# A recurrent layer with routed experts on one core: three groups of transposes declared float32r, with a float32r identity

## The reference, cut to what matters

```python
xn = _layernorm(x, axis=-1)
s = _L0_attn_ref(xn, ...)      # x@Wx -> conv -> silu -> b, c, dt -> scan -> norm -> * silu(z) -> @Wout
g = _silu(_L0_ffn_ref(xn, ...))
x = x + s * g

# inside _L0_attn_ref, with 8 heads of 64 and a state of 64 x 64 each
decay = jnp.exp(dt_t * a)[..., None, None]
state = decay * state + b_bar[..., None] * x_t[:, :, None, :]
y_t = jnp.einsum('bhn,bhnp->bhp', c_t, state)

# inside _L0_ffn_ref, with 8 experts, each taking its own top 1024 of 8192 tokens
G_t, idx_t = jax.lax.top_k(Sm.T, k)
tokens = xf[idx]
mid = jax.nn.silu(jnp.einsum('keh,ehf->kef', tokens, Wu) + bu)
out = jnp.einsum('kef,efh->keh', mid, W_down) + b_down
y = jnp.zeros_like(xf).at[idx].add(G[..., None] * out)
```

## Time and profile before

| | |
|---|---|
| Median of 3 runs | 1216.25 us (1212.61 to 1216.72) |
| The profiled execution | 1207.71 us, span 1205.9 us |
| TensorE busy | 1181.9 us, 98%, 13979 matmul records |
| Weight loads (PEld) | 973.4 us, beside the matmuls |
| VectorE, GpSimd, ScalarE busy | 79%, 64%, 54% |
| Start of the first transpose | 9.05 us (its weight load) |
| End of GpSimd's first wait in phase_front | 9.57 us |
| DMA | 214.84 MB, mean 178 GB/s |

### The profile page before, as it was taken

How to read it: one execution, slowest core, us unless ns; L and a number is a source line. 1 busy time by engine, 2 the same in 40 slices (tenths; PEclk the granted TensorE clock), 3 DMA queues, 4 the chain that set the end, 5 groups by cost and what they waited for, 6 DMA issues and landing times.

```text
span 1205.9 us, 35027 instructions
## 1 busy us (share of the span) xinstructions
PE 1181.9 (98%) x13979; PEld 973.4 (81%) x13979; DVE 947.5 (79%) x2272; ACT 653.2 (54%) x1406; POOL 774.4 (64%) x726
## 2 busy tenths in 40 slices
PE   9999999999999999999999998999999999999998
PEld 4566668888888878888878787888888888899998
DVE  7999975899987778777778778987767676777676
ACT  5999985454445444444444445455445443545444
POOL 4888945555455667666766658566766645577674
PEclk9999999999999999999999999999999999999999
DMA  9698774544343444443443346555544436799994
GB/s 304 242 360 324 281 277 133 115 154 122 132 148 124 149 126 122 134 144 120 131 140 129 120 126 199 159 151 97 119 92 106 81 80 133 272 333 318 333 333 164
DMA packets 122450, 214.84 MB, mean 178 GB/s; under 512 B 22448, under 2 KB 80560, under 8 KB 117552
## 3 DMA queue, kind: packets, MB, share of 16 engines
q1 hardware_dynamic: 109136, 195.32, 48.1%
q0 software_dynamic: 12288, 17.05, 8.4%
q10 hardware_dynamic: 864, 0.24, 0.1%
HBM read 131.03 MB, written 81.53 MB: 176 GB/s over the span
## 4 chain that ended last, share of the span: by engine, by line
PE 85%; DVE 5%; ACT 2%; DMA 2%; issue 2%; SPq 1%; POOL 1%; ACTq 0%; POOLq 0%; DVEq 0%
PE ps L1406 27%; PE ps L1772 10%; PE ps L2282 8%; PE ps L2261 7%; PE ps L2046 6%; PE ps L1496 3%; PE ps L1418 3%; PE ps L2048 3%; PE ps L1485 3%; PE ps L1473 3%; PE ps L1508 2%; PE ps L1428 2%; PE ps L682 2%; PE ps L630 2%; DMA x_dram<-x 1%
## 5 line engine op out<-in xcount | busy, mean ns | idle before, releaser
L1956 POOL DMA_INDIRECT ffn_dram<-ob,idx x64 | 108.6, 1697 | 83.5 <-DVE ob L1875 68.3
L1356 ACT ACTIVATE decay<-tap,ncum 128x64 f32<-128x64 f32 x344 | 87.0, 335 | 126.7 <-POOL tap L1257 122.3
L1262 POOL TENSOR_TENSOR x_lo<-x,x_hi 128x512 fp32r<-128x512 f32 x56 | 77.3, 1380 | 76.3 <-ACT x_hi L1335 76.3
L1285 POOL TENSOR_SCALAR yb<-x,dcol 128x512 f32<-128x512 f32 x64 | 44.9, 703 | 108.5 <-DMA y_dram<-yb 61.4
L2046 PE MATMUL ps<-dn,mid_hi 128*128 128x512 f32 x288 | 104.8, 399 | 0.5 <-DVE moments L1846 0.5
L2004 ACT ACTIVATE mid<-ps,b_up 128x512 f32<-128x512 f32 x96 | 65.9, 690 | 66.8 <-PE ps L1772 61.4
L1406 PE MATMUL ps<-x_hi,w_hi_b 128*128 128x512 f32 x240 | 99.4, 414 | 0.0
L1406 PE MATMUL ps<-x_hi,w_hi_c 128*128 128x512 f32 x240 | 98.2, 409 | 0.0
L2137 POOL TENSOR_SCALAR yc<-yc,gn_scale,gn_shift 128x512 f32<-128x512 f32 x56 | 77.6, 1397 | 30.9 <-DMA yc<-y_dram 30.9
L1406 PE MATMUL ps<-x_lo,w_hi_b 128*128 128x512 f32 x240 | 94.4, 393 | 0.0
L557 POOL TENSOR_TENSOR acc<-acc,tap 128x512 f32<-128x512 f32 x64 | 82.4, 1291 | 18.0 <-DVE acc L298 13.9
(11 more groups left out here) (327 smaller groups left out, 3853.7 us busy)
## 6 DMA issues: line engine op xcount, KB each, us to landing
x_dram<-x SPq DMA_DIRECT2D x16, 1024.0 KB, 5.6
yc<-y_dram SPq DMA_DIRECT2D x16, 1024.0 KB, 6.7
y_dram<-yb SPq DMA_DIRECT2D x30, 512.0 KB, 3.5
x<-x_dram SPq DMA_DIRECT2D x26, 512.0 KB, 4.8
tap<-cum_half_dram SPq DMA_DIRECT2D x86, 128.0 KB, 3.0
tap<-cum_dram SPq DMA_DIRECT2D x86, 128.0 KB, 3.2
rows_dram<-xn SPq DMA_DIRECT2D x16, 512.0 KB, 3.3
ffn_dram<-zero SPq DMA_DIRECT2D x64, 128.0 KB, 4.1
```

What stands on the lines that cost most here:

```text
L1262: nc.gpsimd.tensor_tensor(x_lo[b % 2][:, m, :], x2[b % NX][:, m, :], x_hi[b % 2][:, m, :].bitcast(F32), ALU.subtract).then_inc(x_lo_ready, 1)
L1356: n = nc.scalar.activation(decay[g % 2][:, h, :], key_row[g % NR][:, h, :], ACT.Exp, bias=t.ncum[:, g, h:h + 1])
L1956: pool.indirect_dma_start(out=t.ffn_dram, out_offset=bass.IndirectOffsetOnAxis(ap=t.idx[:, e, h * HC + c:h * HC + c + 1], axis=0), in_=ob[ ...
```

## The change

The transposes of three tiles go through a new helper that passes the tile and the PSUM output as float32r, with an identity of type float32r: x in the scan, the gathered rows, and the rows read back by the output. These tiles are filled by loads alone. For x in the scan that takes a separate name for the front's x2, x2_early, at the same addresses, since the front writes that one with ScalarE. The identity becomes a tile of its own, loaded by a DMA from GpSimd's queue (float32 in DRAM to a float32r tile) with a semaphore of its own. The other transposes use the same tile read as float32. The constants tile is shorter by the identity, and its columns are renumbered.

```diff
+def turn_tile(pe, out, tile, ident):
+    return pe.transpose(out.bitcast(F32R), tile.bitcast(F32R), ident)

 # phase_front
-        x2 = t.x2
+        x2 = t.x2_early
-            act.dma_start(t.ident, ins["const"][:, C_ID:C_ID + P]).then_inc(ident_wx_loaded, 16)
+            pool.dma_start(t.ident_r, ins["const"][:, C_ID:C_ID + P]).then_inc(ident_loaded, 16)
-            act.wait_ge(ident_wx_loaded, 32)
+            act.wait_ge(wx_loaded, 16)
-            pe.wait_ge(ident_wx_loaded, 32)
+            pe.wait_ge(wx_loaded, 16)
+            pe.wait_ge(ident_loaded, 16)
             first_turn()
-            sp.dma_start(t.cst[:, C_ID + P:C_END], ins["const"][:, C_ID + P:C_END]).then_inc(cst_loaded, 16)
+            sp.dma_start(t.cst[:, :], ins["const"][:, 0:C_END]).then_inc(cst_loaded, 16)
 # phase_scan, turn_x
-                mm = pe.transpose(ps_xb[:, m * P:(m + 1) * P], x2[b % NX][:, m, c * P:(c + 1) * P], t.ident)
+                mm = turn_tile(pe, ps_xb[:, m * P:(m + 1) * P], x2[b % NX][:, m, c * P:(c + 1) * P], t.ident_r)
 # expert_parts, turn
-                mm = pe.transpose(ps_t(u)[k][:, c * P:(c + 1) * P], xg[q][:, c, k * P:(k + 1) * P], t.ident)
+                mm = turn_tile(pe, ps_t(u)[k][:, c * P:(c + 1) * P], xg[q][:, c, k * P:(k + 1) * P], t.ident_r)
 # output_parts, turn
-                mm = pe.transpose(o.ps_t[k][:, c * P:(c + 1) * P], o.xn[p][:, c, k * P:(k + 1) * P], t.ident)
+                mm = turn_tile(pe, o.ps_t[k][:, c * P:(c + 1) * P], o.xn[p][:, c, k * P:(k + 1) * P], t.ident_r)
 # build
-        t.ident = t.cst[:, C_ID:C_ID + P]
+        ident = sb("ident", [P, P], F32R)
+        t.ident_r, t.ident = ident[:, :], ident[:, :].bitcast(F32)
+            with ExitStack() as early:
+                t.x2_early = [early.enter_context(nc.sbuf_tensor(f"x2_early{i}", [P, s.MT, BLK], F32)) for i in range(2)]
```

More of the change, by code:

```diff
@@ L19 @@
 EPS = 1e-5
-C_ID, C_TRI, C_LATER, C_RSUM, C_RTRI, C_IOTA, C_HEAD, C_TAU, C_PIDX, C_LO, C_BIT = (
-    0, 128, 256, 384, 512, 640, 768, 896, 960, 961, 969)
+C_TRI, C_LATER, C_RSUM, C_RTRI, C_IOTA, C_HEAD, C_TAU, C_PIDX, C_LO, C_BIT = (
+    0, 128, 256, 384, 512, 640, 768, 832, 833, 841)
 BITS = 30
[L25 to L29, removed]
+C_EPS = 890
+C_MID, C_HIGH, C_ONE = 891, 892, 893
+C_DOWN, C_DHIGH = 894, 895
+C_END = 896
+C_SEL, C_ID, C_ALL = C_END, C_END + 32, C_END + 32 + P
 class Shapes:
@@ L129, in phase_front @@
         top, esum, einv = (a[:, :].unsqueeze(2) for a in (inv, rstd, nmr))
-        cst_loaded, ident_wx_loaded, small_loaded, late_loaded, half_loaded = (
-            sem(f"a_{n}_loaded") for n in ("cst", "ident_wx", "small", "late", "half"))
+        cst_loaded, wx_loaded, small_loaded, late_loaded, half_loaded = (
+            sem(f"a_{n}_loaded") for n in ("cst", "wx", "small", "late", "half"))
+        ident_loaded = sem("a_ident_loaded")
         x_loaded = [sem(f"a_x_loaded{i}") for i in range(NX)]
@@ L529, in _ @@
             for m in range(MT):
-                nc.scalar.activation(t.x_hi[1][:, m, :], x2[1][:, m, :], ACT.Copy).then_inc(x1_hi, 1)
+                nc.scalar.activation(t.x_hi[1][:, m, :], t.x2[1][:, m, :], ACT.Copy).then_inc(x1_hi, 1)
             act.wait_ge(ten, 2)
@@ L590, in _ @@
                 pool.wait_ge(x1_hi, m + 1)
-                nc.gpsimd.tensor_tensor(t.x_lo[1][:, m, :], x2[1][:, m, :], t.x_hi[1][:, m, :].bitcast(F32),
+                nc.gpsimd.tensor_tensor(t.x_lo[1][:, m, :], t.x2[1][:, m, :], t.x_hi[1][:, m, :].bitcast(F32),
                                         ALU.subtract).then_inc(x1_lo, 1)
@@ L771, in _ @@
             sp.dma_start(xin[0][:, 2:CH, :], x_blk[0][:, 2:CH, :]).then_inc(half_loaded, 16)
-            sp.dma_start(wx[:, :, :], ins["wx"].rearrange("(k p) n -> p k n", p=P)).then_inc(ident_wx_loaded, 16)
+            sp.dma_start(wx[:, :, :], ins["wx"].rearrange("(k p) n -> p k n", p=P)).then_inc(wx_loaded, 16)
             load_x(1)
-            sp.dma_start(t.cst[:, C_ID + P:C_END], ins["const"][:, C_ID + P:C_END]).then_inc(cst_loaded, 16)
+            sp.dma_start(t.cst[:, :], ins["const"][:, 0:C_END]).then_inc(cst_loaded, 16)
             sp.dma_start(select, ins["const"][:, C_SEL:C_SEL + PAIR]).then_inc(cst_loaded, 16)
@@ L801, in _ @@
                     sp.wait_ge(thin_ready, b + 2)
-                    sp.dma_start(x2[b % 2][:, :, :], t.x2_dram[b % 2]).then_inc(x2_back[b % 2], 16)
+                    sp.dma_start(t.x2[b % 2][:, :, :], t.x2_dram[b % 2]).then_inc(x2_back[b % 2], 16)
             for p in range(2):
```

## The result

| | median us | lowest | highest | runs |
|---|---|---|---|---|
| before | 1215.69 | 1212.61 | 1217.51 | 6 |
| changed | 1209.22 | 1207.10 | 1210.41 | 6 |

The ratio is 0.9947, with an interval of 0.9931 to 0.9962. So the change is faster by 6.5 us, where I forecast 14.4 us (1202 us). The profiled executions don't show this by themselves: the one after took 1209.23 us, about its median, the one before 1207.71 us, which is 8 us under its own. Single stages have to be compared, not the two spans.

The account below looks back on a forecast made before the run. TensorE's instruction distances were taken to bound the kernel. Savings of 10.0 us (scan), 5.0 (experts) and 0.9 (output), 15.9 together, less 0.9 and 0.6, gave 14.4 us off the 1216.25 us median: 1202 us, range 1197 to 1219 us.

Parts of the forecast that it names:

- The bound: In scan, experts and output, time is the sum of distances between TensorE's instructions; TensorE is busy 98% of 1205.9 us.
- The failed step: Each of 408 transposes in scan, experts and output falls from 109 to 70 ns, saving 39 ns, together 15.9 us.
- the ends that I gave: Bounds for one float32r transpose's distance: 56 ns, saving 21.6 us over 408, to 120 ns, adding 4.5 us.
- the milder form of rival 1: Load and columns disturb each other: 80 ns per transpose, 11.8 us less 1.1, 1205.5 us; counted within the forecast's 0.62.
- The missing term: Claim that counts and order on TensorE stay and only the cost of one transpose changes.
- My deductions of 0.9 + 0.6 us: Gain not on the path: 0.9 us at the scan's end, 0.6 us in the nine waits before L1485.
- Rival 1: The float32r weight load sets the pace: a transpose costs up to 6 ns more, 1218 us at most; chance 0.17.
- Rival 2: Nothing changes, the transpose mode keeps two cycles per column: 1216 us, or 1220.8 us with float32r extra; chance 0.14.
- Rival 3: Transposes' loads are not hidden: load plus columns make 162 ns each, 21.6 us more, 1238 us; chance 0.07.
- Rival 4: The identity is late by up to 2 us, shifting any case; no chance of its own.
- cost nil: Identity load on GpSimd's queue, occupying it 1.07 us, lands at 4.5 us, before TensorE needs it at 9.05 us.
- The signs I named: Transpose records about 225 ns, eight in 0.55 us, projections unchanged, scan waits growing under 2 us, first transpose about 9.05 us.

Follow-up runs that it names:

- experiment 6: Changed kernel with each of the scan's 256 float32r transposes issued twice: 1222.35 us, ratio 1.0115 to the kernel before, 18.8 us over the changed kernel.
- experiment 4: Changed kernel with the last transpose of each of 83 float32r groups back in float32: 1201.06 us, ratio 0.9937 to the kernel before.
- experiment 5: Changed kernel with the first transpose of each of 83 groups, not the last, in float32: 1203.73 us, ratio 0.9966 to the kernel before.
- experiment 7: Short streams and pairs of float32 and float32r transposes and ordinary matmuls issued on the identity ahead of the first transpose: one run of 1216.67 us.
- experiment 2: Changed kernel with all transposes float32 again, keeping the separately loaded identity and x2_early: 1208.33 us, ratio 1.0003 to the kernel before.
- experiment 3: Changed kernel with float32r only in the scan's transposes, gathered rows and output float32: 1204.89 us, ratio 0.9974 to the kernel before.
- experiment 1: Changed kernel unedited on two further chips, against the kernel before: 1202.81 us against 1207.54 (ratio 0.9954) and 1203.59 against 1208.81 (0.9961).

## Why the prediction was right and wrong

**The bound** was right. TensorE's distances made the time: issuing more of them added nearly their whole sum (experiment 6), and no other engine took over.

**The failed step** is the price of one transpose: "I take 70 ns, slightly above, since at 128 columns less time is left for the load behind the matmul". The line through 512 and 256 columns was right for the columns: with its load done ahead, a float32r transpose takes 58 to 67 ns. But in a group it takes 85, but for the first two of eight. The load of the next one no longer starts with the matmul before it. It starts 50 ns into that matmul's record, and the next matmul follows 35 ns after it: 85. Whether the late start makes the 85 ns, or the load itself can't be done faster than that, stays open: the pairs r and f (171) and f and wide (197) are the sums of 85 and 85 and of 85 and 112 ns, as a load's own pace would have it, but r and wide (216) is not. Of the ends that I gave, 56 and 120 ns, it is about the middle, and the milder form of rival 1 with 80 ns was nearest. What that costs: the groups shrank by 64 x 0.12 + 16 x 0.24 + 3 x 0.24 = 12.2 us, not by 15.9. That milder form had 11.8 us here. This step alone would have made the forecast 12.2 - 1.5 = 10.7 us in place of 14.4.

**The missing term** is larger: "What changes is the cost of one". I counted the projections, and all that follows, as unchanged, and kept no bound for it. The first float32r matmul behind a group lost 71 ns. The trace has it behind 77 of the 83 groups, 5.5 us; of the other six, four run directly into other transposes, one stands ahead of a 64 x 64 product (197 ns for 196) and one ahead of a wait. That this matmul pays because of the form just ahead of it is shown by experiments 4 and 5 from both sides. The reason that I give for it is argued: the 109 ns of a float32 transpose just covered an ordinary operand's load, which by the pace of wide is 113 ns at most; 64 ns of columns and a later start do not. 12.2 - 5.5 = 6.7 us, against 4.7 to 6.5 measured on three chips. My deductions of 0.9 + 0.6 us for what isn't on the path are small beside this, and no run tests them by themselves. That 1209 us lies inside my range of 1197 to 1219 us says nothing for the mechanism, since the range was drawn to hold the case of no change.

The Trainium skill's page "TensorE: Matmul & The Clock Gate" (Step-by-step: what each phase is for) says that TensorE can pull a weight load ahead of the matmuls still running. The trace agrees: behind a float32 transpose and behind float32r matmuls of 256 and 512 columns the next load starts within 4 ns of the start of the record. In the streams of float32r transposes and of 128-column float32r matmuls it comes some 50 ns later (experiment 7).

**Rival 1** (the load sets the pace) was right in its kind: the 85 ns are more than the columns take, and the load is what the rows show beside them. Its price in the strong form was wrong, since the load stays at 140 ns in the records and not at 188; by that form nothing would have been gained. **Rival 2** (nothing changes) falls with the records, 242 to 257 ns for 272 to 286. **Rival 3** (loads not hidden) holds in part: a part of the load's time stands outside the columns, but the distance is 85 ns, not 162. **Rival 4** and my "cost nil" for the identity: the load occupied GpSimd for 0.76 us, not the 1.07 that I took, and experiment 2 shows no cost.

**The signs I named.** Records of about 225 ns: they are 242 to 257 on the mean, and 221 to 230 only for the first two of a group of eight, whose load was ahead. Eight in 0.55 us: 0.63. "Projections should keep their lengths": 2.85 for 2.77 us, and this was the sign of what I had left out. Waits grow under 2 us: by 1.4. The first transpose's weight load at 9.05 us: at 8.71.

## What to carry to other kernels

When an instruction gets shorter, the one behind it can pay for it, as here by 71 ns: look at the weight load of the instruction after a group, and price it once per group. The pace read from wide shapes (66 ns from 512 and 256 columns) held here only where the load was done ahead. Where a group of short float32r transposes stands ahead of a matmul with a long load, leaving the last one float32 was worth 71 - 47 = 24 ns per group here (the last transpose costs 132 ns for 85), 2.0 us over 83 groups by that sum and 1.75 us by the medians, whose intervals overlap.

## What was not expected of the hardware

- In a stream of float32r transposes, and as well in one of ordinary 128-column float32r matmuls, the next weight load starts some 50 ns after the start of the matmul's record; behind a float32 transpose it starts with it (timeline of experiment 7).
- A 128-column ordinary float32r matmul repeated takes 113 ns, more than the 82 to 85 ns of a float32r transpose of the same size; its load is the longer one, 192 against 140 ns in the records.
- A float32r transpose with its load done ahead takes 58 to 67 ns for 128 columns, near the 53 ns of one cycle per column, and its load has the length of a float32 transpose's, 140 ns in the record against 188 of ordinary float32r operands and 98 of bf16 ones.
- In the first profile after, the clock fell to its lower level in parts of 736 to 760 us; before's profile and those of experiments 2, 3, 5 and 6 have 1.00 from 740 to 760 us, those of experiments 1, 4 and 7 have 0.91. With 7 of 14 runs of the changed kernel under 1.0 against 7 of 36 of the kernel before, the change seems to make such falls likelier; why, no run tells. In experiment 1 the changed kernel's runs at 0.997 took 3.6 to 4.0 us more than the medians of its runs at 1.0.
